# Window attention on one core: transposing the exponentiated scores, or making the scores a second time already transposed

## The reference

```python
q, k, v = ...                                   # 1x1 convolution of gn(x); 64 windows of 7x7, 12 heads of 16
dots = einsum('wnid,wnjd->wnij', q, k) * 16 ** -0.5 + bias[None]
attn = softmax(dots, axis=-1)
out = einsum('wnij,wnjd->wnid', attn, v)
x = x + conv1x1(out, w_proj) + b_proj
x = x + depthwise_5x5(displace(gn(x)))          # separable, so two matrix products per plane
```

## Time and profile before

| | us |
|---|---|
| median of 3 runs | 6754.12 |
| lowest, highest | 6752.31, 6755.74 |
| profiled execution, own time | 6760.54 |
| its span | 6758.8 |
| VectorE busy | 5226.7 (77%) |
| TensorE matmul busy | 4955.8 (73%) |
| ScalarE busy | 4669.7 (69%) |
| GpSimd busy | 3211.1 (48%) |

### The profile page before, as it was taken

How to read it: one execution, slowest core, us unless ns; L and a number is a source line. 1 busy time by engine, 2 the same in 40 slices (tenths; PEclk the granted TensorE clock), 3 DMA queues, 4 the chain that set the end, 5 groups by cost and what they waited for, 6 DMA issues and landing times.

```text
span 6758.8 us, 233050 instructions
## 1 busy us (share of the span) xinstructions
PE 4955.8 (73%) x81476; PEld 3795.1 (56%) x81476; DVE 5226.7 (77%) x11722; ACT 4669.7 (69%) x15619; POOL 3211.1 (48%) x3428
## 2 busy tenths in 40 slices
PE   5777777877777777778777777767787777777776
PEld 4555555655555555556555555555565555555554
DVE  4888777887778887778877788877787777878784
ACT  3777666776667776667766677766677666777673
POOL 1355444554445554445544455544455444555454
PEclk9998889988889988889888899988898888989897
DMA  3545556455555455554555554555545555545554
GB/s 80 111 102 116 112 115 121 102 114 114 112 118 118 104 116 113 115 121 101 116 115 111 117 120 103 115 113 114 121 104 114 115 110 117 119 102 112 114 111 76
DMA packets 1368966, 750.78 MB, mean 111 GB/s; under 512 B 1182938, under 2 KB 1256666, under 8 KB 1363546
## 3 DMA queue, kind: packets, MB, share of 16 engines
q1 hardware_dynamic: 1367770, 735.06, 52.6%
HBM read 156.66 MB, written 154.14 MB: 46 GB/s over the span
## 4 chain that ended last, share of the span: by engine, by line
SPq 27%; DVE 21%; PE 17%; issue 14%; POOL 7%; ACT 6%; DMA 5%; DVEq 1%; POOLq 0%; ACTq 0%
SPq L390 9%; SPq L384 6%; DMA xt<-in_x 4%; SPq L454 4%; SPq L421 4%; ACT prob L774 3%; DVE den L980 3%; DVE pT L989 3%; SPq L403 3%; PE pTr L571 3%; POOL probn L1191 2%; DVE qks L942 2%; DVE mx L966 2%; PE pO L589 2%; DVE mix L942 2%
## 5 line engine op out<-in xcount | busy, mean ns | idle before, releaser
L1191 POOL TENSOR_TENSOR probn<-prob,den 128x588 f32<-128x588 f32 x1024 | 1199.9, 1172 | 2512.4 <-DVE den L985 2348.5
L589 PE MATMUL pO<-pT,vv 98*32 98x49 f16 x36864 | 772.6, 212 | 1312.1 <-DVE pT L989 889.7
L774 ACT ACTIVATE prob<-pS,mx 128x49 f32<-128x49 f32 x4096 | 1178.7, 305 | 600.3 <-DVE mx L965 589.3
L589 PEld LDWEIGHTS pO<-pT,vv 98*32 98x32 f16 x36864 | 666.6, 138 | 1534.6 <-DVE pT L989 822.4
L989 DVE SCALAR_TENSOR_TENSOR pT<-pTr,pT 98x588 f16<-98x588 f32 x1024 | 754.7, 737 | 839.4 <-DMA xt<-in_x 374.8
L571 PE MATMUL pTr<-cst,probn 128*98 128x128 f32 x6144 | 987.6, 303 | 22.1 <-POOL probn L1191 21.5
L787 ACT ACTIVATE pT<-pTr 98x588 f16<-98x588 f32 x1024 | 684.2, 668 | 426.3 <-PE pTr L571 422.1
L774 ACT ACTIVATION_READ_ACCUMULATOR prob<-pS,mx 128x1 f32 x4096 | 853.1, 208 | 0.0
L552 PE MATMUL pS<-biasT,addb 128*64 128x196 f16 (+1 forms) x4096 | 602.0, 324 | 258.6 <-ACT prob L774 191.2
L571 PEld LDWEIGHTS pTr<-cst,probn 128*98 128x98 f32 x6144 | 714.2, 140 | 56.2 <-POOL probn L1191 29.2
L559 PE MATMUL pS<-kst,qst 96*64 96x98 f16 x12288 | 690.5, 221 | 0.0
(11 more groups left out here) (186 smaller groups left out, 14841.7 us busy)
## 6 DMA issues: line engine op xcount, KB each, us to landing
kst<-qks SPq DMA_DIRECT2D x1536, 98.0 KB
qst<-qks SPq DMA_DIRECT2D x1536, 49.0 KB, 1.9
kst<-mix SPq DMA_DIRECT2D x768, 98.0 KB
vv<-cv SPq DMA_DIRECT2D x1024, 73.5 KB
out<-xr SPq DMA_DIRECT2D x256, 294.0 KB
xr<-x_scratch SPq DMA_DIRECT2D x64, 882.0 KB
x_scratch<-xm SPq DMA_DIRECT2D x128, 392.0 KB, 3.0
xm<-in_x SPq DMA_DIRECT2D x32, 1176.0 KB, 14.9
```

The costliest lines, as they stand in the source:

```text
L589: mm = pe.matmul(pO[r:r + 32, p % 2, hp // 4, NT * win:NT * win + NT], vv[:, g % 2, win, p % PPR, a, hp::NHP], pT[0:98, p % 2, b, 2 * hp + ...
L774: a = act.activation(prob[:, p % 2, t], pS[:, 0, t], ACT.Exp, bias=mx[:, p % 2, h:h + 1], scale=-1.0, accum_out=den[:, p % 2, h:h + 1])
L1191: pool.tensor_tensor(heads(probn[:, p % 2, :]), heads(prob[:, p % 2, :]), spread(den[:, p % 2, :], NT), ALU.mult).then_inc(S["norm_p"], 1)
```

## The change

- `scores` makes positive scores, six heads to each PSUM bank. `maximum` is one reduction over 12 heads.
- `turn` now transposes only the 12 maxima of each row into a corner of `pT` (one 32-bit transpose). `shift_hi` (ScalarE) and `shift_lo` (VectorE) split them into rows of `mov`, whose other rows hold a constant pattern.
- `shifted` (TensorE, new) makes the scores a second time, transposed: six matmuls with `biasT` stationary and `mov` moving add bias and minus the maximum, twelve add k·q.
- `exp` (ScalarE) is one exponential over 98x588 out of PSUM. `prob_hi` (VectorE) copies it to 16 bits, `prob_lo` (GpSimd) makes the remainder.
- `attend` uses both parts, and 12 further matmuls with a matrix of ones (`onesb`) give the row sums, repeated in each head's partitions. `inverse` takes the reciprocal of these 128x196 sums, `normalize` (VectorE) multiplies into `osb`, and `out_hi`, `out_lo` and `out_low` (now GpSimd for `om`) split that.
- `direct`, `subtract`, `denominators`, `turned_hi`, `turned_lo` and GpSimd's multiplication are gone.
- VectorE's waits for `x1_p` and `x_in` stand just ahead of the statistics that need them, at a step's end, and no longer at its start. The k buffers have another layout, and the six `qst` transfers of the mixed rest carry twice the bytes.

```diff
@@ TensorE
+                if due("exp_a", i, p):
+                    pe.wait_ge(S["exp_a"], nth("exp_a", i, p))
+                pe.transpose(pT[0:NH, 1, 384:512], mx[:, :], const("ident")).then_inc(S["mt_pe"], 1)
+
+            def shifted(i, p):
+                c, q = divmod(p, PPC)
+                pe.wait_ge(S["mh_a"], nth("mh_a", i, p + 1))
+                pe.wait_ge(S["ml_d"], nth("ml_d", i, p + 1))
                 for hp in range(NHP):
-                    mm = pe.transpose(pT_[0:98, 128 * hp:128 * hp + 128],
-                                      probn[:, p % 2, 98 * hp:98 * hp + 98], const("ident"))
-                mm.then_inc(S["t_pe"], 1)
+                    bank, at = hp // 3, PW * (hp % 3)
+                    pe.matmul(pT[0:98, bank, at:at + PW], biasT[:, PW * hp:PW * hp + PW], mov[:, :],
+                              start=(hp % 3 == 0), stop=False, skip_group_check=True)
+                    for win in (0, 1):
...
+                        mm = pe.matmul(pT[0:98, bank, a:a + NT], kst[:, c % 2, hp, PW * w:PW * w + PW],
+                                       qst[:, c % 2, t:t + NT], start=False, stop=True,
+                                       skip_group_check=True)
+                mm.then_inc(S["st_pe"], 1)
@@ attend
+                for hps in (range(4), range(4, NHP)):
+                    for k, b in enumerate((probh, probl)):
+                        for hp in hps:
+                            r, at = 32 * (hp % 4), PW * (2 + hp // 4)
+                            mm = pe.matmul(pO[r:r + 32, at:at + PW], onesb[:, :],
+                                           b[0:98, p % 2, PW * hp:PW * hp + PW],
+                                           start=(k == 0), stop=(k == 1), skip_group_check=True)
@@ ScalarE
+                act.activation(banked(prob[0:98, p % 2, :]), pT[0:98, :, 0:HB], ACT.Exp).then_inc(S["exp_a"], 1)
+            def shift_hi(i, p):
+                act.wait_ge(S["mt_pe"], nth("mt_pe", i, p + 1))
@@ VectorE
+            def prob_hi(i, p):
                 dve.wait_ge(S["exp_a"], nth("exp_a", i, p + 1))
...
+                dve.tensor_copy(probh[0:98, p % 2, :], prob[0:98, p % 2, :]).then_inc(S["ph_d"], 1)
             def inverse(i, p):
-                dve.wait_ge(S["sum_d"], nth("sum_d", i, p + 1))
-                dve.reciprocal(den[:, p % 2, :], den[:, p % 2, :]).then_inc(S["rden_d"], 1)
+                dve.wait_ge(S["o_pe"], nth("o_pe", i, p + 1))
+                dve.reciprocal(rden[:, :], pO[:, 2 * PW:4 * PW]).then_inc(S["rden_d"], 1)
@@ GpSimd
+            def prob_lo(i, p):
+                pool.wait_ge(S["ph_d"], nth("ph_d", i, p + 1))
+                pool.tensor_tensor(probl[0:98, p % 2, :], prob[0:98, p % 2, :], probh[0:98, p % 2, :],
+                                   ALU.subtract).then_inc(S["pl_p"], 1)
```

More of the change, by code:

```diff
@@ L56 @@
 WSC = 256.0
-PSC = 1024.0
+MSC = 64.0
+MROWS = 12
 ASC = 64.0
@@ L244, in par, with q_at, slots @@
             return (i.base + (i.shift + 2)) % 2
+        def q_at(hp, w):
+            return CHUNK * hp + NT * w if hp < 4 else 4 * CHUNK + 2 * CHUNK * (hp - 4) + PW * w
+        def slots(ap, rows, part, odd, half):
+            a = PW * (PPC * half)
+            return ap[rows, part, a:a + 2 * ROW].rearrange("p (w e j) -> p w e j", e=2, j=NT)[:, :, odd, :]
         def windows(ap):
@@ L563, in scores @@
+                        for hp in range(NHP // 2 * bank, NHP // 2 * bank + NHP // 2):
+                            at = PW * (hp % (NHP // 2))
+                            o = pS[64 * win:64 * win + 64, bank, at:at + PW]
+                            t = q_at(hp, w)
+                            mm = pe.matmul(o, qst[:, c % 2, t:t + 64], kst[:, c % 2, hp, PW * w:PW * w + PW],
+                                           start=False, stop=True, skip_group_check=True)
                 mm.then_inc(S["s_pe"], 1)
@@ L630, in body @@
                         attend(i if p >= 2 else i - 1, (p - 2) % PAIRS)
+                    if att:
+                        turn(i, p)
+                    if att if p < PAIRS - 1 else nxt:
+                        scores(i + (p + 1) // PAIRS, (p + 1) % PAIRS)
                     b = blur_step(p, 12, prev)
@@ L633, in body @@
                         blur(i - 1, b, 0)
-                    if p >= 1 and att or p < 1 and prev:
-                        turn(i if p >= 1 else i - 1, (p - 1) % PAIRS)
                     if nxt and p in (13, 17):
@@ L816, in body @@
                 for p in range(PAIRS):
+                    if p >= 1 and att or p < 1 and prev:
+                        exp(i if p >= 1 else i - 1, (p - 1) % PAIRS)
+                    if att:
+                        shift_hi(i, p)
                     v = before(v_step, p, prev, att, nxt)
@@ L865, in _ @@
             then(dve.memset(tabs[:, 1, :], 0.0))
-            dve.wait_ge(S["const_in"], 13 * 16)
+            dve.wait_ge(S["const_in"], 16 * 16)
             ri = xm[:, 1, 0:NT * NT].bitcast(I32)
-            then(dve.tensor_scalar(hot[0][:, 0:NT * NT], ri, const("iota")[:, 0:1], None, ALU.is_equal))
-            then(dve.tensor_scalar(hot[1][:, 0:NT * NT], ri, const("iota")[:, 1:2], None, ALU.is_equal))
+            first, last = MROWS * NT, (MROWS + NT) * NT
+            for half in (0, 1):
+                then(dve.memset(hot[half][:, 0:first], 0.0))
+                then(dve.tensor_scalar(hot[half][:, first:last], ri, const("iota")[:, half:half + 1], None,
+                                       ALU.is_equal))
             then(dve.tensor_copy(tabh[:, 0, :, :], tabs))
@@ L1039, in body @@
                     if p >= 2 and att or p < 2 and prev:
-                        turned_lo(i if p >= 2 else i - 1, (p - 2) % PAIRS)
+                        inverse(i if p >= 2 else i - 1, (p - 2) % PAIRS)
+                    if att:
+                        shift_lo(i, p)
+                    if p >= 2 and att or p < 2 and prev:
+                        normalize(i if p >= 2 else i - 1, (p - 2) % PAIRS)
                     if prev and p == 5:
```

308 lines of the change are left out of this document (145 added, 163 removed).

## The result

| | before | after |
|---|---|---|
| median of 4 runs, us | 6754.93 | 8671.2 |
| lowest, highest, us | 6752.31, 6760.95 | 8639.39, 8686.68 |
| profiled span, us | 6758.8 | 8637.5 |
| granted TensorE clock, mean | 0.888 | 0.778 |

The changed kernel takes 1.283 times the time of the one before, 95% interval 1.279 to 1.287. The changed kernel's profiled execution, at 8639.39 us, is the fastest of its four runs.

What follows compares the result with a forecast made beforehand. A serial loop through three engines was to bound steps 12 to 27: plus 29.6, minus 5, minus 5.5, so +19 us per image over 31 images, 7345 us from 6760.5. Own range 7150 to 7650, wider range 6635 to 7850.

Steps and rivals of the forecast that it cites:

- Prices: Times taken for the new instructions: reciprocal 1.38 us, maximum 0.76, `prob_hi` copy 0.47, exponential 0.67, `normalize` 0.36, `shift_lo` 0.25.
- The rival with the reciprocal at 0.42 us: VectorE's reciprocal has a fixed extra cost, so it is cheap: about 6635 us, faster than before; chance 11%.
- VectorE's sum per pair: VectorE's added work per pair, 3.04 us, against 2.99 us removed, so VectorE is not relieved.
- The copy that waits for GpSimd: Rival: sharing SBUF interfaces, VectorE's `prob_hi` takes 0.77 us instead of 0.47: 7570 us, inside the own range; no separate chance.
- The loop: Steps 12 to 27: a serial chain through TensorE, ScalarE and VectorE, 117.6 us against 88.0, plus 29.6 us per image.
- a rival of 15%: TensorE's clock falls in the loop's gaps: +18 us per image in steps 12 to 27, +4 elsewhere, 8030 us; 15%.
- the first loop: The loop whose attention has no blur beside it; left as it was, with no change in time.
- Steps 28 to 31 and 0: Steps without blur, with `y`, blur product 0 and normalize out of the loop: 26.6 us against 27.5 + 4.2, minus 5.
- Steps 1 to 11: SyncE's 59.5 us bounds steps 1 to 7; step 9 begins about 63 us after step 1; steps 9 to 11 unchanged.
- the 5.5: Us saved per image because the load's landing is waited for at step 8's end, behind its attention.
- What would show it: Signs named beforehand: reciprocal about 1.38 us, steps 12 to 27 near 118 us, VectorE and TensorE both under 80% busy.
- VectorE as the bound: Rival: the loop isn't closed and a blur step costs VectorE's sum, about 5.3 us: 6340 us; chance 9%.

Runs made afterwards that it cites:

- kernel 3: The changed kernel with VectorE's `y` moved ahead of `prob_hi` and the reciprocal, behind the maximum: 7812.08 us, 1.154 of before.
- kernel 10: The changed kernel with a plain copy in place of the reciprocal (division left out) and idle matmuls, 20 in blur steps: 7627.07 us, 1.129 of before.
- kernel 5: The changed kernel with VectorE's `shift_lo` moved ahead of the reciprocal, behind `prob_hi`: 9066.73 us, 1.342 of before.
- kernel 1: The changed kernel with idle matmuls ahead of the scores, 20 in each blur step, 12 in other even steps: 8041.7 us, 1.188 of before.
- kernel 12: The kernel before, with only VectorE's waits for `x1_p` and `x_in` moved to just ahead of the statistics: 6669.69 us, ratio 0.987.

## Why the prediction was wrong, point by point

- **Prices: right, but for one.** Reciprocal 1378 ns for 1.38, and the copy, the maximum, the exponential, `shift_lo` (251) and `normalize` (361) as taken. The rival with the reciprocal at 0.42 us is refuted. `out_lo` was to save 0.18 us a pair and saves 0.06, since its `ot` takes 596 ns where it took 355; so VectorE's sum per pair grew by 0.17 us and not 0.05. The reciprocal's cost grows with the columns. My estimate of some 1.75 us from the Trainium skill's repeat count of 8 ("VectorE: DVE Perf Modes", section "First, the fixed hardware budget") was too high by 0.37 us as a price.
- **The copy that waits for GpSimd: never put to the test by the change.** The copy took 466 ns in the mean, but GpSimd stood idle during 1023 of the 1024 copies; the other took 636. In kernel 3, with `y` at another place, the two do meet: 82 copies lie for more than half of their time beside GpSimd's work and take 722 ns in the mean, where 941 with GpSimd idle take 464 (I had priced 0.77 against 0.47). One of them, with GpSimd's instruction beside it:

```profile
2188.75 1.26 DVE L1009 CAST probh<-prob 98x588 f16<-98x588 f32 x1 [0.28 <-ACT prob L806]
2188.72 0.97 POOL L1167 TENSOR_TENSOR xt<-xt,pjt 64x392 f32 x1 [0.19 <-POOL xm L1167]
```

  So the wait is real, and the rival was right about the copy; its price never fell due in the changed kernel.
- **The loop: right in the main.** Order and sum held at full clock (117.7 for 117.6), and taking `y`, the exponential's place or the reciprocal out of it each gave 495 to 1067 us. Not every term lay wholly in it: at full clock a reciprocal shorter by 16.3 us in 16 steps was worth 6.9 (kernel 10), and `shift_lo` taken from behind it cost time (kernel 5).
- **The step that failed: the clock.** The sum was made with TensorE's durations at full clock, and the fall to half speed was put aside as a rival of 15%, because "none of them is over 2 us". The gaps are 1.8 us in the mean, and the clock fell in them or shortly behind them. The rival's own price was near: +18 us an image in the blur steps, measured 20.6. Its +4 elsewhere was not: the other stretches of kernel 1 take 128.1 us an image and those of the changed kernel 127.1. The clock is the largest of four terms, 639 us of the 1326, but it alone does not save the forecast: with the clock at 1.00 in the blur steps the kernel still takes 8042 us, over the top of the range, and the next two points and the first loop are the rest. The prediction itself had the pieces: a loop that leaves TensorE idle in every step, and the earlier trace rows, where of the five stretches only the one without such gaps had a clock above 0.9. The Trainium skill ("TensorE: Matmul & The Clock Gate", section "Part 1: The HAM clock gate") says that the gate follows how busy the engine was of late. The traces agree: 0.98 where TensorE was busy 80.5 of 88.0 us, 0.76 where it was 109.6 of 142.5, 1.00 where idle matmuls filled it.
- **Steps 28 to 31 and 0: a second miss, 10.6 us an image.** I priced them without blur, at 26.6. But `y` of the last block and its product are made in step 28: 8.4 us in both the changed kernel and kernel 1, where I had 5.7. And step 31 holds a pause at the end of the loop's body: in image 14 none of the five engines has work from 4074 to 4075 us, and before none from 3179 to 3181. It is there in both kernels, here VectorE's first instruction behind it (over all images VectorE's pause is 76.1 us after and 130.5 before, 2.5 and 4.2 a loop):

```profile
4075.97 0.77 DVE L994 TENSOR_REDUCE mx<-pS 128x12 f32<-128x588 f32 x1 [3.00 <-issue]
```
```profile
3181.06 0.77 DVE L989 SCALAR_TENSOR_TENSOR pT<-pTr,pT 98x588 f16<-98x588 f32 x1 [3.88 <-issue]
```

  Before, it was inside the 27.5 us of steps 28 to 31. The sum replaced that window by priced steps and left the pause out: 9.0 us in step 31, where 5.1 was taken. These two make 6.6 of the 10.6; the rest is spread over steps 29, 30 and 0, with no cause shown.
- **Steps 1 to 11: a third, 8.3 us an image.** SyncE's queue is the bound as said, but its stream starts later after the head of step 1. VectorE's `qk_lo` of step 1, the stream's first transfer and its last load in the changed kernel, and VectorE behind its landing:

```profile
3816.44 0.56 DVE L968 SCALAR_TENSOR_TENSOR qh<-pQ,qh 128x392 f16<-128x392 f32 x1
...
3817.02 8.39 SPq L399 DMA_DIRECT2D qst<-qh  x12
...
3866.35 1.33 SPq L470 DMA_DIRECT2D xt<-in_x  x2
```
```profile
3878.25 1.50 DVE L1127 BATCH_NORM_STATS2 gst<-xm 128x6 f32 x3 [4.12 <-DMA xt<-in_x]
```

  From first transfer to landing it is 61.2 us, against 59.5 before. But the stream begins 5.8 us behind the head of step 1 (3811.23), where it was 1.9: it waits for that `qk_lo`, which now stands behind the copy's wait for the exponential and the reciprocal. So step 9 begins 68.8 us after step 1 and not 63, and before it was 68.5: nothing of the 5.5 was gained. Steps 9 to 11 are 20.9 us for 18.6. Kernel 12, where nothing else is changed, shows what the moved wait is worth by itself: 2.9 us, about half of what I gave it.
- **The first loop: a fourth, 55 us once.** "The first and last loops are left as they were" priced the longer attention of the first loop at nothing; it and what comes ahead of it took 55 us more.
- **What would show it.** Named beforehand: "a granted clock under 0.9 in steps 12 to 27 would make the clock the cause". It is 0.79, and kernel 1 shows it for 20.6 of the 39.6 us.

The other rivals: VectorE as the bound (6340) fell by the loop. Whether doubled bytes cost SyncE time is not settled. Steps 1 to 7 take 57.5 us against 62.1, but the wait for the load has left them; steps 1 to 8, which hold it in both, take 68.8 and 68.5. The queue spends 49.3 us from its first transfer to the start of the last load and spent 48.5, and the six `qst` transfers with doubled bytes take 4.83 us where they took 3.79.

What stays open: the pause at the loop's end was read, not tried; so was the later start of SyncE's stream; and no run shows how much of the 10.6 and 8.3 us a mended order would give back.

## What to carry to other kernels

A chain of hand-overs that runs once per step through three engines is a bound of its own, and can be summed from single rows (here it came out at 117.6 for 117.7, in part by luck); but its sum must be made with TensorE's durations at the clock that the gaps leave it, and where a new order opens a gap in every step, the sum at 1.2 GHz belongs beside the one at 2.4. Before a change puts a long wait early in an engine's order, ask what stands behind it there that another engine waits for: here one instruction at another place gave back 859 of 1916 us, and the clock with it. When a measured window is replaced by priced steps, carry over its pauses and the last block of other work that lies in it. And a price read with one engine idle holds only as long as a new order keeps it idle.
